# Maxima products ahead of the scores, and the first root from ScalarE

## The reference

```python
x = L0_attn_x                                  # (4, 512, 256) float32
xn = _layernorm(x, axis=-1)                    # (x - mean) / sqrt(var + 1e-5)
s = _L0_attn_ref(xn, Wq, Wk, Wv, Wo)           # 16 heads of 16, causal softmax
g = _silu(_L0_ffn_ref(xn, wq_gate, s_gate, wq_up, s_up, wq_down, s_down))
x = x + s * g                                  # hidden width 704, silu(gate) * up
```

## Time and profile before

| | |
|---|---|
| median of three runs | 306.1 us |
| the profiled execution, its own time | 305.38 us |
| its span, first to last instruction | 303.7 us |
| TensorE busy | 277.2 us, 91% |
| VectorE busy | 226.6 us, 75% |
| ScalarE busy | 177.0 us, 58% |
| GpSimd busy | 136.6 us, 45% |
| mean granted TensorE clock | 0.985 of full speed |

### The profile page before, as it was taken

One profiled execution on the slowest core, in us unless ns is written; L12 is line 12 of the kernel. 1 busy time (PEld: TensorE's weight loads), 2 busy tenths in 40 slices (PEclk: granted clock), 3 DMA queues, 4 the chain that ended last, 5 costly groups with the idle time before them and its releaser, 6 DMA issues.

```text
span 303.7 us, 5527 instructions
## 1 busy us (share of the span) xinstructions
PE 277.2 (91%) x2040; PEld 191.1 (63%) x2040; DVE 226.6 (75%) x386; ACT 177.0 (58%) x257; POOL 136.6 (45%) x241
## 2 busy tenths in 40 slices
PE   0797995999999998999999999999989998998993
PEld 0585673578656575686857567896656664766462
DVE  5883968694798969958499978758788886679434
ACT  2645449653577888532567787524667776344760
POOL 6007635711268753322358845112467653114361
PEclk9999999899999999999999999999999997999998
DMA  7646569279306530297308320396219020001302
GB/s 263 211 119 198 174 132 218 66 200 150 129 2 124 86 123 21 68 195 166 133 2 158 53 73 1 89 198 148 91 41 189 17 73 2 2 2 37 106 2 70
DMA packets 21470, 31.39 MB, mean 103 GB/s; under 512 B 2612, under 2 KB 10420, under 8 KB 21444
## 3 DMA queue, kind: packets, MB, share of 16 engines
q1 hardware_dynamic: 21028, 30.39, 41.4%
q10 hardware_dynamic: 416, 0.66, 0.6%
HBM read 20.19 MB, written 10.49 MB: 101 GB/s over the span
## 4 chain that ended last, share of the span: by engine, by line
PE 75%; DVE 12%; ACT 5%; DMA 4%; issue 2%; SPq 1%; ACTq 0%
PE ps L690 15%; PE ps L692 12%; PE ps L691 12%; PE ps L898 10%; PE ps L859 9%; PE ps L816 7%; ACT pt L1114 2%; PE ps L906 2%; DMA qk_scratch<-xr 2%; DVE ps L1415 2%; DVE mx L1418 2%; DVE mx L1423 2%; PE ps L915 1%; PE ps L729 1%; DMA xin<-in_x 1%
## 5 line engine op out<-in xcount | busy, mean ns | idle before, releaser
L1114 ACT ACTIVATE pt<-ps 128x1024 f32<-128x1024 f32 x80 | 81.8, 1027 | 43.0 <-PE ps L859 39.2
L1272 POOL TENSOR_SCALAR_AFFINE_SELECT pt<-pt 128x256 f32<-128x256 f32 (+1 forms) x112 | 47.4, 440 | 88.8 <-ACT pt L1114 88.1
L1415 DVE TENSOR_TENSOR ps<-ps,tri 128x512 f32<-128x512 f32 (+1 forms) x72 | 42.7, 593 | 32.7 <-PE ps L816 32.4
L859 PE MATMUL ps<-qp,kp 50*128 50x512 f32 (+3 forms) x256 | 40.1, 373 | 4.3 <-ACT pt L1114 4.3
L1240 POOL TENSOR_TENSOR hl<-hid,hh 128x512 fp32r<-128x512 f32 (+1 forms) x24 | 30.8, 1283 | 25.8 <-ACT hh L1059 25.7
L1418 DVE TENSOR_REDUCE mx<-ps 128x2 f32<-128x1024 f32 x32 | 39.1, 1225 | 3.3 <-PE ps L830 2.3
L898 PE MATMUL ps<-pt,vt 128*17 128x512 f32 (+3 forms) x480 | 41.1, 444 | 0.0
L1233 POOL TENSOR_TENSOR hid<-hid 128x512 f32<-128x512 f32 (+1 forms) x24 | 30.8, 1285 | 20.7 <-DVE hid L1393 16.1
L816 PE MATMUL ps<-kp,qp 48*128 48x512 f32 (+3 forms) x256 | 35.9, 339 | 4.1 <-DMA kp<-qk_scratch 2.1
L859 PEld LDWEIGHTS ps<-qp,kp 50*128 50x128 f32 x256 | 20.4, 186 | 29.2 <-issue 15.9
L1420 DVE TENSOR_REDUCE mx<-ps 128x2 f32<-128x768 f32 x32 | 30.7, 958 | 2.4 <-PE ps L830 1.4
(11 more groups left out here) (146 smaller groups left out, 574.8 us busy)
## 6 DMA issues: line engine op xcount, KB each, us to landing
qk_scratch<-hid SPq DMA_DIRECT2D x24, 256.0 KB
qp<-qk_scratch SPq DMA_DIRECT2D x14, 256.0 KB, 4.5
kp<-qk_scratch SPq DMA_DIRECT2D x14, 256.0 KB, 6.5
qp<-qk_scratch SPq DMA_DIRECT2D x18, 128.0 KB, 5.0
kp<-qk_scratch SPq DMA_DIRECT2D x18, 128.0 KB, 6.7
xr<-in_x SPq DMA_DIRECT2D x4, 512.0 KB, 4.0
out<-xr SPq DMA_DIRECT2D x8, 256.0 KB, 2.2
xin<-in_x SPq DMA_DIRECT2D x3, 512.0 KB, 7.2
```

What stands on the lines that cost most here:

```text
L859: mm = nc.tensor.matmul(ps[:, base + e, c:c + T - j * P], kp[part, place(b, half), col, j * P:(j + 1) * P], qp[part, place(b, half), col, ...
L1114: nc.scalar.activation(pt[:, 2 * kk:2 * kk + 2, :], ps[:, base:base + 2, :], ACT.Exp, scale=SCALE).then_inc(exp_done, 1)
L1272: mm = nc.gpsimd.affine_select(out=diag, in_=diag, compare_op=ALU.is_ge, fill=0.0, base=0, pattern=[[0, diag.shape[1]], [1, P]], channel_m ...
L1415: nc.vector.tensor_tensor(diag, diag, mask, ALU.add).then_inc(tri_added, 1)
```

## The change

It has two parts. In `TENSOR_STEPS`, wherever a step had the scores product and the maxima product side by side with the scores first, the maxima product now stands first; steps where another unit stood between them keep their order where it isn't in the diff. The strings of the other engines stay as they are.

In the head, the first batch's root is computed otherwise. ScalarE takes the square root of the variances, VectorE its reciprocal and then one Newton step in place of the bit trick and three steps. VectorE then makes the product `shf` = -mean / sqrt(variance), with which ScalarE normalises the fourth token tile; VectorE normalises three. ScalarE's high part of the q, k, v weights comes in two pieces (q and k, then v) around that tile. The high part of the gate weights moves behind the two pieces of x, and that of the up weights from ahead of the first q, k chunk to behind the second.

```diff
-    "s.0 m.8 gu.10",
-    "s.1 m.9 >t.0",
-    ">t.1 s.2 m.10",
+    "m.8 s.0 gu.10",
+    "m.9 s.1 >t.0",
+    ">t.1 m.10 s.2",
     "c.1 s.3 >qk.0 m.11 >qk.1",
-    "s.4 m.12",
-    "pv.0 pv.1 s.5 m.13",
+    "m.12 s.4",
+    "pv.0 pv.1 m.13 s.5",
...
-    "s.10 m.18",
-    "<o.1 s.11 m.19",
+    "m.18 s.10",
+    "<o.1 m.19 s.11",
     "s.12",
...
+            def split_qkv_hi(cols):
+                nc.scalar.copy(wh[:, :, cols], raw_qkv.rearrange("p (k n) -> p k n", k=KD)[:, :, cols]).then_inc(wh_done, 1)
+
+
+            act_e.wait_ge(ln_step, TT + 1)
+            nc.scalar.activation(nw[:, 1, :], nw[:, 0, :], ACT.Sqrt).then_inc(sqrt_done, 1)
             act_e.wait_ge(wqkv_loaded, 32)
-            nc.scalar.copy(wh[:].rearrange("p k n -> p (k n)"), raw_qkv).then_inc(wh_done, 1)
+            split_qkv_hi(slice(0, 2 * D))
+            act_e.wait_ge(first_shift, 1)
+            nc.scalar.activation(xn[:, TT - 1, :], xin[:, TT - 1, :], ACT.Identity, scale=nw[:, 1, TT - 1:],
+                                 bias=shf[:, TT - 1:]).then_inc(xn_done, 1)
+            split_qkv_hi(slice(2 * D, 3 * D))
...
-            split_gu_hi(0)
             split_x(0, 0)
             split_x(0, 1)
+            split_gu_hi(0)
+            chunk_hi(0, 0)
+            chunk_hi(0, 1)
             split_gu_hi(1)
-            for c in range(4):
-                chunk_hi(0, c)
+            chunk_hi(0, 2)
+            chunk_hi(0, 3)
...
             def first_root():
-                ln(nc.vector.tensor_scalar(nwi[:, 0, :], v.bitcast(I32), 1, None, ALU.logical_shift_right))
-                ln(nc.vector.tensor_scalar(y.bitcast(I32), nwi[:, 0, :], -1.0, MAGIC, ALU.mult, ALU.add))
+
+                dve.wait_ge(sqrt_done, 1)
+                ln(nc.vector.reciprocal(y, y))
...
             first_root()
-            for _ in range(NEWTON):
-                newton()
-            for i in range(TT):
+            newton()
+            nc.vector.scalar_tensor_tensor(shf[:], mv[:, :, 0], -1.0, y, ALU.mult, ALU.mult).then_inc(first_shift, 1)
+            for i in range(TT - 1):
                 normalise(0, i)
...
             for k in range(KD):
                 split_x(0, k)
+            dve.wait_ge(wh_done, 2)
             split_qkv_lo(slice(2 * D, 3 * D))
```

More of the change, by code:

```diff
@@ L48 @@
 TENSOR_STEPS = (
-    "s.0 m.8 gu.10",
-    "s.1 m.9 >t.0",
-    ">t.1 s.2 m.10",
+    "m.8 s.0 gu.10",
+    "m.9 s.1 >t.0",
+    ">t.1 m.10 s.2",
     "c.1 s.3 >qk.0 m.11 >qk.1",
-    "s.4 m.12",
-    "pv.0 pv.1 s.5 m.13",
[L55 to L71, removed]
-    "<z2.1 s.3 c.1 m.11 >qk.0",
[L73 to L118, removed]
-    "s.10 m.18",
@@ L120 @@
-    "<o.1 s.11 m.19",
+    "m.12 s.4",
+    "pv.0 pv.1 m.13 s.5",
+    ">qk.2 >qk.3 m.14 s.6 dn.0",
+    "pv.2 c.2 m.15 s.7 dn.1",
+    "m.16 s.8 >gu.0",
+    ">gu.1 pv.3 m.17 s.9 >gu.2 pv.4",
+    "m.18 s.10 >gu.3",
+    "zt.0 m.19 s.11 pv.5",
+    ">gu.4 >m.0 s.12",
+    "pv.6 c.3 >gu.5 >m.1 s.13",
+    ">gu.6 >m.2 s.14 >gu.7 zt.1",
+    ">m.3 s.15 pv.7 z2.0 pv.8",
+    ">m.4 s.16 >gu.8",
+    "zt.2 >m.5 s.17 pv.9",
+    ">gu.9 >m.6 s.18 >c.0",
+    ">gu.10 >m.7 s.19",
+    "<pv.10 v.0 m.8 s.0 <pv.11",
@@ new lines @@
+    "v.1 m.9 s.1 >t.0 <zt.3",
+    "m.10 s.2 >t.1 pv.0",
+    "<z2.1 s.3 c.1 m.11 >qk.0",
+    "m.12 s.4 >qk.1",
+    "pv.1 m.13 s.5",
+    "pv.2 <o.0 m.14 s.6 dn.0 >qk.2",
+    "m.15 s.7",
+    "pv.3 >qk.3 m.16 s.8 c.2 >gu.0",
+    "m.17 s.9 pv.4 <o.1",
+    "dn.1 >gu.1 m.18 s.10",
+    "zt.0 >gu.2 m.19 s.11 pv.5 >gu.3",
+    ">gu.4 >m.0 s.12 c.3 pv.6",
+    ">m.1 s.13",
+    ">gu.5 >m.2 s.14 zt.1",
+    ">gu.6 >m.3 s.15 >gu.7",
+    "z2.0 >m.4 s.16",
+    "pv.7 >gu.8 >m.5 s.17 pv.8",
+    ">gu.9 >c.0 >m.6 s.18",
@@ new lines @@
+    "zt.2 pv.9 >m.7 s.19",
+    "gu.10 <pv.10 m.8 s.0",
+    "<pv.11 v.0 m.9 s.1 v.1",
+    ">t.0 >t.1 m.10 s.2 pv.0",
+    "c.1 <zt.3 >qk.0 m.11 s.3 >qk.1",
+    "<z2.1 m.12 s.4 dn.0",
+    "m.13 s.5 dn.1",
+    "m.14 s.6 <o.0 >qk.2 >qk.3 pv.1",
+    "m.15 s.7",
+    "<o.1 m.16 s.8 c.2",
+    ">gu.0 m.17 s.9 pv.2 >gu.1",
+    ">gu.2 zt.0 m.18 s.10",
+    "pv.3 >gu.3 m.19 s.11",
+    "pv.4 >gu.4 >m.0 s.12 c.3 >gu.5",
+    ">m.1 s.13",
+    "pv.5 >gu.6 >m.2 s.14 zt.1",
+    ">gu.7 >m.3 s.15 pv.6 z2.0 pv.7",
@@ L121 @@
+    ">m.4 s.16 >gu.8",
+    "pv.8 >m.5 s.17 >gu.9",
+    ">m.6 s.18",
+    "zt.2 >c.0 >gu.10 >m.7 s.19 pv.9",
+    "<pv.10 m.8 s.0 <pv.11",
+    "v.0 m.9 s.1 v.1",
+    "m.10 s.2",
+    "<zt.3 m.11 s.3 c.1",
+    "pv.0 m.12 s.4",
+    "dn.0 m.13 s.5 <z2.1",
+    "pv.1 m.14 s.6",
+    "dn.1 m.15 s.7 c.2 pv.2",
+    "m.16 s.8",
+    "pv.3 m.17 s.9 <o.0",
+    "m.18 s.10",
+    "<o.1 m.19 s.11",
     "s.12",
@@ L521, in build @@
         first_pack = sem("first_pack_loaded")
+        sqrt_done, first_shift = map(sem, ("sqrt_done", "first_shift"))
         pv_first = sem("pv_first")
```

## The result

| | before | changed |
|---|---|---|
| median of 20 runs each | 306.15 us | 308.7 us |
| lowest to highest | 304.06 to 309.46 | 306.48 to 311.83 |
| ratio, 95% interval | | 1.0061 [1.0038, 1.0085] |

The ratio leaves out executions over 1.5% above the fastest of their kernel (four of the changed kernel's 20, its slowest, and one of before's), so it gives 1.9 us where the medians differ by 2.5. By the ratio the time is 308.0 us, close to the upper end of my range of 304.0 to 308.4; the median of all 20 runs, 308.7, lies just above that end. The difference of 0.6% is just more than the 0.5% that I counted as none. It went the way of rival 2.

A forecast was written before the change was run, and what follows sets the result against it. TensorE's own work was taken to bound the middle, with idle time at both ends. The terms -0.9 + 0.8 + 0.3 - 0.3 + 0.6 = +0.5 us gave a forecast of 306.5 us, range 304.0 to 308.4.

The forecast's parts named there:

- rival 2: Hand-over to batch 0: a longer wait ahead of m.10 brings one more half-clock fall, +1.7, 308.2 us; chance 0.22.
- a third stretch at half clock: Sign against the forecast: TensorE's clock falls to half in three stretches, where before had two.
- TensorE's waits between 66 and 250 us: Sign against the forecast: these waits in the middle together differ from before by more than 1 us.
- Term 1: Head, the root: fewer VectorE instructions and three tiles instead of four make x ready 1.28 us earlier.
- Terms 2 and 3: Head: the gain passes through gate weights, q, k chunks and DMA to the first maxima product, -0.9 us.
- Term 4: Head, second table load before the first tanh: tanh about 0.5 us later, covered by TensorE's slack, so 0.
- Term 5: Hand-over to batch 0: s.2 goes 1.04 us later behind m.10, delaying its exponential and s.3; +0.8 us.
- Term 6: First down product at 65.16: VectorE's low part of the down weights comes later, behind s.5's exponential; +0.3 us.
- The middle: Batch 2: c.1's wait of 0.82 us for VectorE shrinks because m.9 is 0.34 earlier; -0.3 us.
- The end: Batch 3: step 11's scores go 0.57 us later behind m.19, shifting all that follows; +0.6 us.
- Rival 1: Hand-over: packed k lands early, m.10 doesn't wait, the first clock fall stays away; -2.6, 303.5 us; chance 0.22.
- Rival 3: Head: late q, k, v weights delay the fourth tile, so the root brings 0 instead of -0.9; 307.4 us; chance 0.08.

The follow-up runs named there:

- filled kernel before: Six idle matmuls ahead of the first maxima product, in the kernel before: 305.91 us, ratio 0.9985.
- head alone: The changed kernel with the order of products of the kernel before: 305.39 us, ratio 0.9992.
- both back: The changed kernel with step 2 of batches 0 and 2 and batch 3's twelve steps in the order of before: 305.00 us, ratio 0.9972.
- changed filled: The changed kernel with eight idle matmuls in the wait ahead of the first maxima product: 307.91 us, ratio 1.0079.
- batch 3 back: The changed kernel with the order of before in the twelve steps of batch 3 that have both products: 307.03 us, ratio 1.0027.
- old root: The changed head and the order of before, with the first root computed as before, without square root or second table load: 305.88 us, ratio 0.9999.
- order alone: The kernel before with the changed TENSOR_STEPS and its own head: 308.76 us, ratio 1.0123.
- step 2 alone: The kernel before with one swap, m.10 ahead of s.2 in step 2 of batch 0: 306.93 us, ratio 1.0025.
- step 2 put back: The changed kernel with s.2 ahead of m.10 again in step 2 of batch 0: 306.92 us, ratio 1.0039.
- The changed head in the order of before, filled: The changed kernel with the order of before and six idle matmuls ahead of the first maxima product: 304.93 us, ratio 0.9930.

## Where the prediction was right, and where it was off by a little

**Forecast and sign.** "No change" had 0.56, "slower" 0.22. The measured +0.6% is slower, just past the bound. The range held for the ratio (308.0 us) and not for the median of all runs (308.7), so that it held is in part luck. Two of the signs that I had named as showing the forecast wrong came: a third stretch at half clock, in the first execution, and TensorE's waits between 66 and 250 us, which rose from 1.5 us to 3.3 in the second execution. Of these 1.8 us 0.9 is the wait ahead of the first down product, which before lay ahead of this stretch. The other 0.9 cost nothing that can be seen: the stretch to step 7 is as long as before (202.98 against 202.90 in the filled kernel before).

- **Term 1, right.** x at 8.50 (8.33 foreseen), against 9.76 before; the square root took 0.20, where I took 0.25.
- **Terms 2 and 3, right.** The low part of the gate weights starts at 12.48, the chunk follows at 14.16 (14.3 foreseen), and `m.0` gains 0.93 (0.9 foreseen). The wait for the DMA was not steady, though, as shown below for `m.0`.
- **Term 4, right.** The load of 1.28 stands at 18.66 (18.2 foreseen) and no wait of TensorE for ScalarE lies ahead of `m.0`. The Trainium skill's page "ScalarE: Activation LUTs" (What ACT_TABLE_LOAD costs) adds a drain of about 1.38 us behind each switch. No such gap is here: the load ends at 19.94 and the tanh starts at 19.96. What the term missed lies outside the span: the 0.36 us above.
- **Term 5, right.** `s.2` at 50.22 and `s.3` at 51.97 (51.9 foreseen), against 49.28 and 51.20 with the head alone: 0.94 and 0.77 later, where the sum had 1.04 and 0.8.
- **Term 6, right.** The first down product waits 0.92 us, +0.32 on the earlier trace rows. Terms 5 and 6 together were to cost 1.1 and cost 1.1 (37.85 - 36.76), though by the row of both back they divide into about 0.5 and 0.6, where I had 0.8 and 0.3.
- **The middle, missed.** I counted -0.3 at `c.1` in batch 2. Its wait is 0.96, not shorter than the 0.82 of the earlier trace rows. VectorE was only 0.2 earlier against TensorE, and its cast ahead of the shift took 1.02 where it had taken 0.70. The term should have been 0. The cast and the transposition in the second execution:

```profile
222.84 1.02 DVE L1453 CAST cn<-mx 128x16 fp32r<-128x16 f32 x1
...
225.24 0.30 PE L837 MATMUL ps<-ident,cn 128*128 128x128 f32 x1 [0.96 <-DVE cn L1455]
```

- **The end, right.** +0.52 where I had +0.6: the scores behind wait 1.12 instead of 0.55.

The terms as measured: -0.9 + 1.1 + 0 + 0.5 = **+0.7 us**, where I had +0.5. With the 0.36 outside the span the fixed cost is **+1.1 us**. I had carried the profiled execution's 1.7 us above its span over unchanged. That sum alone, 0.35%, would still be no change.

**The step that failed** is that the sum left the clock as it was, and put a further fall into rival 2 at 0.22. Of the 2.6 us between the means, 1.1 is the fixed cost, 0.7 is more time at half rate, and the other 0.8 is that the same half-rate time costs more. Rival 2 had the size (308.2 us) and the direction. Its cause, the long wait ahead of `m.10`, isn't shown. The wait was over 2 us in four kernels, and over 2 us was to decide. In three of them (changed filled 2.03, changed in its first execution 2.28, batch 3 back 2.34) the fall at the hand-over lasts 6.8 us. It lasts as long in head alone, old root, before filled and both back, where `m.10` doesn't stand first and no gap there is over 1.45 us. Only the order alone, with 2.33, has 10 us. The longer fall near 255 us stands in step 2 alone and batch 3 back, which both have the order of before in batch 3. So what the traces show is falls of changing length at the same two places. That the order makes them more frequent rests on the mean half-rate times (12.1 to 13.3 us in the three kernels with all swaps, 7.8 to 10.9 in the others), and through which wait it does so stays open. My count against rival 2, that a part lies over idle time, held for the first 3.4 us more (0.46) and not for the next (1.5).

**What I hadn't looked at: `m.0`.** The wait ahead of it differs between executions with an unchanged head. The first execution of the changed kernel:

```profile
12.34 0.42 PE L743 MATMUL ps<-xh,wl 128*128 128x512 f32 x1
...
28.32 0.50 PE L817 MATMUL ps<-kp,qp 48*128 48x512 f32 x2 [2.80 <-DMA kp<-qk_scratch]
```

The kernel with step 2 put back:

```profile
11.98 0.40 PE L743 MATMUL ps<-xh,wl 128*128 128x512 f32 x1
...
28.21 0.49 PE L817 MATMUL ps<-kp,qp 48*128 48x512 f32 x2 [3.03 <-DMA kp<-qk_scratch]
```

In both, the q and k products run at full rate (0.40 to 0.42) from 11.8 and 12.3 us on, while both back and head alone still need 0.63 there (12.20 and 12.29). TensorE is then done earlier, the DMA isn't, and TensorE waits 2.8 to 3.0 us instead of 1.4 to 1.5. In these two executions the clock fell behind the wait, and in none with a wait of 2.3 us or less. The changed kernel with its wait filled started as early (0.40 at 11.70), but its wait was cut to 1.07 and no fall followed.

The Trainium skill's page "TensorE: Matmul & The Clock Gate" (HAM oscillation) holds a long idle gap responsible for such falls. `m.0` agrees with that in kind, though the gaps of 2.8 and 3.0 us are shorter than those the page speaks of; so is the wait of 2.3 us for which I had drawn on it in rival 2. The hand-over doesn't agree: there the clock fell in every kernel, before too, where no gap was over 1.31 us.

**Rival 1 fell** with `m.10`'s wait: the fall stayed, and in the second execution came earlier. **Rival 3 fell** too: x was ready 1.26 us earlier; with the old root `m.0` gains nothing, with the new one 0.9.

**A better version.** The changed head in the order of before, filled, ran at 304.93, a ratio of 0.993 to the kernel before and 1.2% under the changed one's median. The fill's share in it isn't shown. Without it the head alone had 305.39 and both back 305.0, the latter with an interval just under 1. What the traces show is the head's 0.9 us at `m.0`. Less the 0.36 outside the span that leaves about half a microsecond with the order of before, and these runs can't tell so little from none.

## What to carry to other kernels

On an engine that takes its work strictly in order, swapping two neighbours is free where both are ready. Where the one moved ahead waits for something the other doesn't need, the other is late by what that wait exceeds its own, and by the product itself (here 0.94 us for a wait of 1.87). Look for just these places (the first use of a DMA's data, the last steps with nothing left to fill in) and leave them out of a change that is made everywhere. Where the clock falls for a stretch after idle time, put it into the sum with a price and not only into a rival, and compare medians of many runs sorted by their half-rate time, since two executions of one kernel differed by 4.3 us here (311.83 and 307.52). And compare the time with the span in both kernels: a part of the change can lie outside every row.

## What the runs showed of the hardware

In the 14 profiled executions the stretches at 1.2 GHz ahead of the last microseconds are 3.4, 6.8 or, once, 10.2 us long. Their place and length differ between two executions of one and the same kernel. A fall of 3.4 us costs 0.4 to 1.1 us where part of it lies over idle time, and 0.9 to 1.6 where TensorE is bound. The changed kernel's 20 runs show 6.7 to 17.3 us at half rate, with 306.5 to 311.8 us of time.

When TensorE first reaches full rate in the head also differs between executions (11.7 to 14.3 us in kernels that have x ready at the same time). The two that rose early and had no fill waited 2.8 and 3.0 us for the DMA later and then fell to half rate: of the two executions of the changed kernel, the one that rose earlier ended slower (311.83 against 307.52).

The square root on ScalarE came with 0.36 us more time outside the span, in 104 executions with it against 133 without. The second table load took 1.28 us, and the next activation started 0.02 us behind it.
